# Row maxima as stacked high and low halves: one 64-column product per head in place of two 128-column products per two heads

## What is computed

```
scores = jnp.einsum('bqhd,bkhd->bhqk', q, k) * scale
scores = jnp.where(allowed[None, None], scores, -jnp.inf)
attn = jax.nn.softmax(scores, axis=-1)
out = jnp.einsum('bhqk,bkhd->bqhd', attn, v)
```

## Time and profile before

| what | value |
|---|---|
| median of 3 runs | 480.66 us (478.96 to 481.72) |
| time of the profiled execution | 480.37 us |
| its span, first to last instruction | 478.6 us |
| mean granted TensorE clock | 0.956 |
| busy PE | 406.1 us (85%) |
| busy PEld (weight loads) | 272.9 us (57%) |
| busy DVE / ACT / POOL | 290.9 / 206.2 / 179.2 us |
| L661, 512 products | 39.2 us busy, mean 219 ns |
| L657, 512 products | 25.6 us busy, mean 193 ns |

### The profile page before, as it was taken

The page is one execution under the profiler, slowest core; times in us unless marked ns, Lnnn a source line. Parts: engine busy times, 40 slices in busy tenths (PEclk is TensorE's granted clock), DMA queues, the critical chain, the costliest instruction groups (busy, mean ns, idle before and its releaser), DMA issues. The chain is left out here.

```text
span 478.6 us, 14438 instructions
## 1 busy us (share of the span) xinstructions
PE 406.1 (85%) x4869; PEld 272.9 (57%) x4869; DVE 290.9 (61%) x1178; ACT 206.2 (43%) x502; POOL 179.2 (37%) x305
## 2 busy tenths in 40 slices
PE   0787999999999999999999961599998999999830
PEld 0455777777776677777777640245555555555420
DVE  5575454667756667666675647256665666666614
ACT  0465455445554555554455530044444444444420
POOL 5444433454454554555544345003222222223220
PEclk9999999999999999999999995599999999999975
DMA  7556755444455444423223700211110111111008
GB/s 203 134 142 175 213 136 151 112 112 139 144 165 135 120 120 142 121 66 82 51 53 85 258 14 32 71 42 36 45 38 28 29 43 37 31 34 34 18 16 251
DMA packets 91624, 46.14 MB, mean 96 GB/s; under 512 B 56410, under 2 KB 89852, under 8 KB 91554
## 3 DMA queue, kind: packets, MB, share of 16 engines
q1 hardware_dynamic: 88562, 40.50, 31.8%
q0 software_dynamic: 2272, 4.46, 2.5%
q10 hardware_dynamic: 720, 0.26, 0.2%
HBM read 33.67 MB, written 11.98 MB: 95 GB/s over the span
## 5 line engine op out<-in xcount | busy, mean ns | idle before, releaser
L1097 DVE TENSOR_REDUCE mrow<-ps 128x4 f32<-128x512 f32 x64 | 44.2, 691 | 73.9 <-PE ps L604 73.9
L1303 POOL TENSOR_SCALAR_AFFINE_SELECT amat<-amat 128x512 f32<-128x512 f32 x64 | 42.1, 657 | 119.6 <-ACT amat L819 119.3
L1325 POOL DMA_INDIRECT results<-qas,mrowid x39 | 38.1, 978 | 126.2 <-ACT qas L879 123.1
L747 PE MATMUL ps<-wgl,rest 128*128 (+1 forms) x156 | 75.3, 605 | 4.7 <-DVE hT L1186 4.1
L830 ACT ACTIVATE pmat<-ps 128x512 f32<-128x512 f32 x64 | 38.2, 597 | 67.6 <-PE ps L661 67.6
L819 ACT ACTIVATE amat<-ps 128x512 f32<-128x512 f32 x64 | 38.2, 597 | 27.9 <-PE ps L616 27.9
L1186 DVE TENSOR_TENSOR hT<-ps,kv_tok 128x512 f32<-128x512 f32 x39 | 27.0, 691 | 26.5 <-issue 14.6
L747 PEld LDWEIGHTS ps<-wgl,rest 128*128 128x128 f32 x156 | 26.9, 192 | 27.9 <-issue 27.9
L732 PE MATMUL ps<-w,rest 128*128 (+1 forms) x78 | 42.1, 623 | 0.0
L661 PE MATMUL ps<-identb,mneg 128*128 128x128 bf16 x512 | 39.2, 219 | 0.0
L1264 POOL DMA_INDIRECT routed<-routed_row,slot x32 | 32.6, 1018 | 14.0 <-issue 5.8
(11 more groups left out here) (161 smaller groups left out, 834.7 us busy)
## 6 DMA issues: line engine op xcount, KB each, us to landing
qa_parts<-wgl SPq DMA_DIRECT2D x12, 256.0 KB, 3.1
ks<-k_parts SPq DMA_DIRECT2D x32, 96.0 KB
qas<-qa_parts SPq DMA_DIRECT2D x32, 96.0 KB
xin<-routed SPq DMA_DIRECT2D x39, 72.0 KB, 1.9
ks<-k_parts SPq DMA_DIRECT2D x32, 64.0 KB
qas<-qa_parts SPq DMA_DIRECT2D x32, 64.0 KB
w<-in_W SPq DMA_DIRECT2D x2, 1024.0 KB, 5.4
wgl<-in_Wg SPq DMA_DIRECT2D x2, 1024.0 KB, 6.3
```

The lines of the kernel that those rows point to most:

```text
L747: t = mm(ps[:, GL, :], zxT[:, k % 2, s, :], rhs(wgl[:, bass.ds(e, 1), s, :]), start=(s == 0), stop=(s == 1))
L1097: v.tensor_reduce(mrow[:], ps[:, SQ, :].rearrange("p (a k) -> p a k", k=CH), AX.X, ALU.max).then_inc(max_done, 1)
L1303: q.affine_select(out=amat[:, u % 2], in_=amat[:, u % 2], compare_op=ALU.is_ge, fill=0.0, base=0, pattern=[[0, 4], [1, CH]], channel_multi ...
L1325: q.indirect_dma_start(results, bass.IndirectOffsetOnAxis(mrowid[:, m:m + 1], 0), yw[:, m, :], None, bounds_check=RESULTS - 1, oob_is_err= ...
```

## The change

The high and the low part of a head's maxima (64 queries) now share one column of `mneg`: one of them in rows 0 to 63, the other in rows 64 to 127. The moving operand is minus the 64 x 64 identity, twice, one above the other, so one product adds up both parts with the sign turned, 64 columns wide. There are 8 products a unit as before, each half as wide. DVE writes the two parts in four instructions over 64 rows in place of two over 128; two of them write into the other half of the rows.

```diff
-    c["identb"] = np.eye(128, dtype=np.float32).astype(bf)
+    c["minusid"] = np.tile(-np.eye(WINDOW, dtype=np.float32), (2, 1)).astype(bf)
...
-        mneg = sb("mneg", [128, 2, 2, 4], BF16)
+        mneg = sb("mneg", [128, 2, 4, 2], BF16)
...
-                    for pr in range(4):
-                        for part in range(2):
-                            t = mm(ps[:, ST, pr * CH:(pr + 1) * CH], mneg[:, u % 2, part, pr:pr + 1].to_broadcast([128, 128]), identb[:],
-                                   start=False, stop=(part == 1), skip_group_check=True)
+                    for hh in range(8):
+                        t = mm(ps[:, ST, hh * WINDOW:(hh + 1) * WINDOW], mneg[:, u % 2, hh // 2, hh % 2:hh % 2 + 1].to_broadcast([128, 128]), minusid[:],
+                               start=False, stop=True, skip_group_check=True)
                     t.then_inc(st_ready, 1)
...
-                v.tensor_scalar(mneg[:, b, 0], mrow[:], -1.0, None, ALU.mult).then_inc(nh_done, 1)
-                dve.wait_ge(nh_done, n + 1)
-                v.scalar_tensor_tensor(out=mneg[:, b, 1], in0=mrow[:], scalar=-1.0, in1=mneg[:, b, 0],
-                                       op0=ALU.mult, op1=ALU.subtract).then_inc(mneg_ready, 1)
+
+                half = [slice(0, WINDOW), slice(WINDOW, 2 * WINDOW)]
+                for r in range(2):
+                    v.tensor_copy(mneg[half[r], b, :, r], mrow[half[r]]).then_inc(nh_done, 1)
+                dve.wait_ge(nh_done, 2 * (n + 1))
+                for r in range(2):
+                    t = v.tensor_tensor(mneg[half[1 - r], b, :, r], mrow[half[r]], mneg[half[r], b, :, r], ALU.subtract)
+                t.then_inc(mneg_ready, 1)
```

More of the change, by code:

```diff
@@ L126, in build @@
         ident = sb("ident", [128, 128])
-        identb = sb("identb", [128, 128], BF16)
+        minusid = sb("minusid", [128, WINDOW], BF16)
         sums = sb("sums", [KR, 2, PR], BF16)
@@ L370, in _ @@
                     sp.dma_start(ks[KP:KR, p, w], con["krows"]).then_inc(s_in, 16)
-            for dst, name in ((identb, "identb"), (sums, "sums"), (statemask, "statemask"), (epslin, "epslin")):
+            for dst, name in ((minusid, "minusid"), (sums, "sums"), (statemask, "statemask"), (epslin, "epslin")):
                 sp.dma_start(dst[:].rearrange("r a f -> r (a f)") if name == "sums" else dst[:], con[name]).then_inc(c_in, 16)
```

## The result

The changed kernel takes 469.12 us in the median, against 480.25 us of the kernel before on the same chip: ratio 0.9746, 95% interval 0.9711 to 0.9780. The profiled execution took 469.5 us (span 467.8), with a mean granted clock of 0.953.

What follows compares the result with a forecast made beforehand. PE's own product order was taken to bound the kernel inside a chunk; 50 units x 0.21 us = 10.5 us off the profiled 480.37 us gave 469.9 us, range 465.0 to 473.6 us.

Steps and rivals of the forecast that it cites:

- What bounds a unit: Inside a chunk, the order of PE's own products is the bound; narrower products at L661 gain 0.21 us a unit.
- the weights set the pace: Rival at L661: weight loads or PE's queue set the pace, products stay 56 ns apart; 480.4 us, chance 0.05.
- Where the gain stays: 50 of 64 units keep 0.21 us, 10.5 us; 13 u = 3 units and chunk 7's first lose it; chance 0.58.
- POOL's chain: At chunk boundaries POOL runs mask, cross products, `rstd2`, scatter without slack, so PE waits 0.21 us longer at L557.
- the rival that they lose it: Rival: u = 0 units lose the gain too, their 0.12 us cover being too thin; 38 units, 472.4 us, chance 0.12.
- The POOL reading: At chunk boundaries, a PE signal falling into the issue of POOL's scatter reaches ACT (`linT`) only after it.
- all 64 units keep it: Rival at the boundaries: `linT`'s late start goes with PE, not POOL; 14.1 us gained, 466.3 us, chance 0.18.
- I cost it at nothing: DVE's two more instructions a unit add 0.12 us, at most 0.33, off the path, so cost nothing.
- the cover of 2 us: Over 2 us lie between unit 54's maxima being ready on DVE and the L657 using them; 0.68 in unit 0.
- My own sign: If L657 now waits for DVE, the DVE instruction pairs were costed too low.
- Slower: Rival: longer PE waits at L557 drop the granted clock, 12 us a fall, two priced; 493.9 us, chance 0.04.
- The number: Forecast time of the changed kernel: 469.9 us, from 480.37 us less 10.5.

Runs made afterwards that it cites:

- pe_only: Kernel before with eight products of 64 columns subtracting the high part alone, DVE's code as before: 459.50 us, ratio 0.9724.
- cols32: Changed kernel with products of 32 columns, so half the queries keep their maximum: 464.37 us in one run, against 464.86 for the changed kernel.
- rows4: Products of 64 columns using the high part alone, with four DVE instructions split by rows (64 x 4 numbers): 471.72 us, ratio 0.9812 to the kernel before.
- cols4: Products of 64 columns using the high part alone, with four DVE instructions split by columns (128 x 2): 468.96 us, ratio 0.9767 to the kernel before.
- stack3: Changed kernel with one DVE copy over all rows in place of the first two: 472.10 us, ratio 0.9783 to the kernel before.
- hi4_swap: Kernel before without the low part: four products of 128 columns, one DVE instruction, scatter moved ahead of `rstd2`: 466.28 us, ratio 0.9686.
- base_again: Kernel before, unedited, run again with its profile on the second group's chip: 472.50 us.
- changed_again: Changed kernel, unedited, run again on the second group's chip: 464.86 us, ratio 0.9828 to the kernel before.

## Why the prediction was right, and where it wasn't

- **What bounds a unit.** Right. PE's order is the bound, and each unit without a wait is 213 ns shorter, for 0.21 predicted. The mean duration fell to 192 ns (193 said), the busy time to 25.5 us (25 said), and the group takes 0.33 us (0.33 said). The rival "the weights set the pace" fell with this, and pe_only shows the gain without DVE's part. cols32 gives its limit: from 64 to 32 columns the starts come only 3.5 ns closer.
- **Where the gain stays.** Right in its sum, 50 units, in part by luck: misses of 0.70 and 0.36 us one way and 1.28 the other. The units at u = 3 lost their gain as said, and 0.70 us more. POOL's chain was not the reason for most of it: from the start of its `amat` to the end of the scatter pass 4.32 us as before, in all chunks from 4 on that have the cross products but chunk 8. But `linT` starts 0.25 us behind the scatter where it started 0.20; why stays open. At the end of chunk 8 the 0.36 us that PE waits for DVE's `state` comes in. Chunk 7 was booked as a loss and gave 1.28 us, since its product now ends before the scatter begins. PE's wait for `winT` is 9.5 us for 10.5 said, 12 times for 13: that is chunk 7. The u = 0 units kept their gain but for 0.07 us in one, though the cover of L690's loads was used up. So the rival that they lose it fell here. (Its 12 units count chunk 7's first twice; with 11 it would have said 472.2 us.)
- **The POOL reading** holds on chips where the kernel before takes 480 to 481 us: in all six traces from these (before, after, rows4, cols4, stack3, hi4_swap) the end of L691 or L690 falls into a scatter 10 or 11 times, and each time `linT` starts after the scatter's end, by 0.07 to 0.67 us. At the boundaries into chunks 7 and 15 the scatter is over by then. There it is an earlier signal that comes late: in the changed kernel the L616 for the next `amat` ends at 144.52 us, the scatter at 144.64, and `amat` starts at 144.95, with `linT` behind it, where elsewhere it starts 0.04 us behind L616. With DVE's maxima this makes three signals of PE, to two engines. That the issue holds them is read from where they fall; on which side they are held isn't shown. In the eight traces from the chips where the kernel before takes 473 us it never waits for that end: `linT` starts 0.22 us or less behind the product. Between before and base_again the stretch of the units differs by 6.6 us, about the 6.5 us between their executions. There the rival "all 64 units keep it" is the right one for PE (pe_only: 13.9 us). So I had taken for a property of the program what goes with the chip. Why the chips differ stays open; no run here tells it.
- **The step that failed** is "I cost it at nothing", with 2 x 0.06 = 0.12 us for the pairs and 0.33 as the upper bound. It measured 0.36 in the median, and the whole four took up to 1.60 us in place of 0.73 where they lie beside the scatter (changed_again). I had priced the distance from two neighbours that begin in the same row; the new ones don't. On the chip of the result the cover of 2 us held but for three short waits. On the second group's chip it did not, and DVE takes back 5.0 of 12.8 us. I read the cover in single units and did not add up DVE's load over a chunk. My own sign, that L657 waits for DVE, showed on both.
- **Slower.** A fall of the clock behind a wait at L557 does occur, once, in stack3's trace, after 1.19 us. It cost about 1.5 us, not 12: the low clock lasted 3.5 us there, and I had priced it from the long stretch behind the attention. That it came from the wait is what its place suggests; it wasn't repeated, and a wait of 1.17 us was followed by none.
- **The number** was within 0.8 us of the median, on that chip. That is partly luck: the misses above cancel, and which chip it ran on decided the rest. On the second group's chip the same edit gives 7.9 us, 0.9828.

## What to carry to other kernels

Price a group of matmuls like these by its columns down to a floor of some 26 ns a product, and expect the gain of a busy engine only where no other chain sets the end. When DVE work is split, split it by columns: each piece that begins in the other half of the rows is as good as serial, some 0.2 us at this size. Look at the longest cases too, not only at the median. And ask of a cover whether it holds over a whole loop: a wait elsewhere that pays for it may be gone on the next chip, or after the next edit.

## What was not expected of the hardware

- Whether a PE signal that falls into the issue of POOL's scatter reaches ACT at once (0.22 us) or only after it (`linT` 1.3 us behind its start) differs between chips, and with it goes the time of the same kernel: 472.5 to 473.4 against 480.3 to 481.3 us.
- The same lateness shows at DVE: 0.39 to 0.70 us behind L604 at eight boundaries of the changed kernel on the chip of the result, 0.04 us where nothing is held.
- DVE instructions of 64 x 4 numbers that begin in another row than their neighbour start 193 to 196 ns apart, those of 128 x 2 that begin in the same row 77 ns.
- Beside POOL's scatter and mask single ones of these DVE instructions last 0.49 to 0.69 us where they usually last 0.16.
- Products of 128 x 32 start 25.9 ns apart, 3.5 ns closer than those of 128 x 64.
- The granted clock stood at 1.2 GHz for only 3.5 us in the attention, in one execution, and was back at full in the next stretch.
